# Cross-attention kernel: later Wo and key-block loads, a zeroed tile on TensorE during the first loads, high products of two row blocks first

## The reference

```
Q = split_heads(x @ Wq + bq);  K = split_heads(ctx @ Wk + bk);  V = split_heads(ctx @ Wv + bv)
scores = einsum('bhqd,bhkd->bhqk', Q, K) / sqrt(32)
attn   = softmax(scores, axis=-1)
c      = einsum('bhqk,bhkd->bhqd', attn, V), heads joined
out    = c @ Wo + bo
result = layer_norm(out + x) * gamma + beta          # eps 1e-5
x: (16, 512, 512) f32      ctx: (16, 77, 512) f32
```

## Time and profile before

| | us |
|---|---|
| median of 3 runs | 618.29 (618.0 to 619.93) |
| the profiled execution, whole | 621.88 |
| its span, first to last instruction | 620.1 |
| TensorE busy | 594.5 |
| VectorE busy | 498.2 |
| GpSimd busy | 443.5 |
| ScalarE busy | 364.0 |

### The profile page before, as it was taken

How to read it: one execution, slowest core, us unless ns; L and a number is a source line. 1 busy time by engine, 2 the same in 40 slices (tenths; PEclk the granted TensorE clock), 3 DMA queues, 4 the chain that set the end, 5 groups by cost and what they waited for, 6 DMA issues and landing times.

```text
span 620.1 us, 12039 instructions
## 1 busy us (share of the span) xinstructions
PE 594.5 (96%) x3336; PEld 432.1 (70%) x3336; DVE 498.2 (80%) x913; ACT 364.0 (59%) x674; POOL 443.5 (72%) x395
## 2 busy tenths in 40 slices
PE   5998799999999999999999999999999999999992
PEld 4876577777777777777777777777777777777562
DVE  5434288888888888888888888888888888888776
ACT  5532155466666666666666666666666666655562
POOL 1264143448888888888888888888888888888785
PEclk9999799999999999999999999999999999999997
DMA  8759968888979898979798988989897989796623
GB/s 304 275 211 223 230 142 223 223 198 195 234 200 212 218 225 216 215 203 231 190 230 206 229 218 197 231 204 228 194 245 191 223 206 228 190 230 169 168 77 128
DMA packets 93392, 129.58 MB, mean 209 GB/s; under 512 B 49936, under 2 KB 49936, under 8 KB 93360
## 3 DMA queue, kind: packets, MB, share of 16 engines
q1 hardware_dynamic: 74016, 93.80, 61.0%
q10 hardware_dynamic: 19344, 35.40, 21.9%
HBM read 53.94 MB, written 24.35 MB: 126 GB/s over the span
## 4 chain that ended last, share of the span: by engine, by line
PE 90%; SPq 4%; DMA 3%; DVE 1%; issue 1%; ACT 0%; DVEq 0%
PE p_q L612 27%; PE p_o L680 27%; PE p_s L644 11%; PE p_v L655 10%; PE p_a L630 6%; PE pk L309 5%; PE p_o L111 3%; DMA z<-nmt 1%; SPq L550 1%; SPq L545 1%; PE p_a L697 1%; DMA k_low<-ktl 1%; PE p_den L663 1%; DMA cx<-in_ctx_t 1%; SPq L491 1%
## 5 line engine op out<-in xcount | busy, mean ns | idle before, releaser
L753 ACT ACTIVATE prob<-p_s 77x512 f32<-77x512 f32 x256 | 143.8, 591 | 107.9 <-PE p_s L644 98.0
L968 DVE TENSOR_REDUCE nm<-p_a 128x4 f32<-128x308 f32 x256 | 117.3, 476 | 57.7 <-PE p_a L630 56.8
L1104 POOL TENSOR_TENSOR cl<-cxt,ch 128x512 fp32r<-128x512 f32 x64 | 83.1, 1298 | 111.3 <-ACT ch L778 111.3
L923 DVE TRANSPOSE_TENSOR_REDUCE part<-prob 96x64 f32<-96x2048 f32 x64 | 146.4, 2287 | 1.6 <-issue 1.3
L768 ACT ACTIVATE qh<-p_q,bq_col 128x512 fp32r<-128x512 f32 x64 | 44.0, 687 | 105.6 <-PE p_q L612 105.6
L612 PE MATMUL p_q<-xl,wqh 128*128 128x512 f32 x256 | 101.2, 395 | 0.0
L612 PE MATMUL p_q<-xh,wql 128*128 128x512 f32 x256 | 101.0, 395 | 0.0
L612 PE MATMUL p_q<-xh,wqh 128*128 128x512 f32 x256 | 101.0, 394 | 0.0
L644 PE MATMUL p_s<-z,ks 97*77 97x512 f32 x256 | 95.8, 415 | 5.2 <-DMA z<-nmt 5.1
L680 PE MATMUL p_o<-woh,ch 128*128 128x512 f32 x240 | 95.4, 397 | 0.2 <-POOL cl L1104 0.2
L680 PE MATMUL p_o<-wol,ch 128*128 128x512 f32 x240 | 94.6, 394 | 0.0
(11 more groups left out here) (126 smaller groups left out, 937.2 us busy)
## 6 DMA issues: line engine op xcount, KB each, us to landing
z<-qh SPq DMA_DIRECT2D x256, 128.0 KB, 3.8
z<-ql SPq DMA_DIRECT2D x124, 128.0 KB, 4.8
xn<-in_x ACTq DMA_DIRECT2D x60, 256.0 KB, 3.3
out_dram<-y SPq DMA_DIRECT2D x60, 256.0 KB, 4.2
xt<-in_x_t ACTq DMA_DIRECT2D x58, 256.0 KB, 4.7
ks<-k_high SPq DMA_DIRECT2D x32, 154.0 KB, 4.7
cx<-in_ctx_t SPq DMA_DIRECT2D x4, 616.0 KB, 5.6
k_high<-kth SPq DMA_DIRECT2D x4, 616.0 KB, 3.6
```

Source lines behind the costliest of these rows:

```text
L753: nc.scalar.activation(prob[0:S2, j, :], p_s[j % 2][0:S2, :], ACT.Exp, scale=SCALE).then_inc(prob_ready, 1)
L923: nc.vector.tensor_reduce(part[:], prob[0:KP, :, :].rearrange("p h (i r) -> p (h i) r", r=DK), AX_X, ALU.add, apply_transpose=True).then_i ...
L968: nc.vector.tensor_reduce(nm[:, t, g.k % 2:HALF:2], p_a[t % 2][:, 0:HC * S2].rearrange("p (h k) -> p h k", k=S2), AX_X, ALU.max, negate=Tr ...
L1104: nc.gpsimd.tensor_tensor(cl[:, i, g.k % NCH, :], cx[:], ch[:, i, g.k % NCH, :].bitcast(F32), ALU.subtract).then_inc(cl_ready, 1)
```

## The change

Wo blocks 0 and 1 are loaded in slot 3 and made ready in slot 4, blocks 2 and 3 in slots 5 and 6 (before: loaded ahead of slot 0 and in slot 2, made ready in slots 1 and 3). The `kb` load of the next batch moves from the second slot of a batch, ahead of z, to its third slot, behind the maxima and `v`. In the first stage DVE sets a tile of 128 x 512 f32 (a part of `y`) to zero, and TensorE multiplies it three times by its own first 128 columns as soon as that is done. The result goes to a bank that the first real product overwrites. For row blocks 0 and 1 TensorE no longer takes the three products of a tile together, but for all six tiles first high x high, which waits for `kv_high` alone, then low weights x high context, then high weights x low context. Row blocks 2 and 3 go as before, with the last two products of a tile exchanged.

```diff
-WO_SLOTS = (1, 3)
+WO_SLOTS = (4, 6)
+WARM = 3
...
+        zeros = y[:, 0, :]
...
+            nc.vector.memset(zeros, 0.0).then_inc(zeros_set, 1)
             for i in range(3 * KC):
                 low(i)
...
-            def k_products(i, kc):
+            def k_products(i, kc, terms=range(3)):
...
-                for n, (w, x) in enumerate(((wkh, cxh), (wkh, cxl), (wkl, cxh))):
+                for n in terms:
+                    w, x = ((wkh, cxh), (wkl, cxh), (wkh, cxl))[n]
...
-            for kc in range(KC):
+            pe.wait_ge(zeros_set, 1)
+            for _ in range(WARM):
+                nc.tensor.matmul(pk[0][:], zeros[:, 0:P], zeros[:], start=True, stop=True)
+            for kc in range(2):
+                for n, ready in ((0, kv_high), (1, kv_low), (2, kv_low)):
+                    for i in range(PK):
+                        if i == 0 and n != 1:
+                            pe.wait_ge(ready, 3 * kc + 2)
+                        if i == 0 and n == 1:
+                            pe.wait_ge(ready, 3 * kc + 1)
+                        if i == 1 and n != 1:
+                            pe.wait_ge(ready, 3 * kc + 3)
+                        k_products(i, kc, (n,))
+            for kc in range(2, KC):
                 for i in range(PK):
...
-            for kc in range(2):
-                load_wo(kc)
-
...
-                if g.k % NCH == 1 and g.back(1 - NCH).valid(NG):
-                    if g.back(1).is_first():
+                if g.k % NCH == 2 and g.back(2 - NCH).valid(NG):
+                    if g.back(2).is_first():
                         sp.wait_ge(kb1_zeroed, 1)
-                    load_kb(g.back(1 - NCH))
+                    load_kb(g.back(2 - NCH))
...
-                if g.back(WO_SLOTS[0] + 1).is_first():
-                    load_wo(2)
-                    load_wo(3)
+                for half in range(2):
+                    if g.back(WO_SLOTS[half] - 1).is_first():
+                        load_wo(2 * half)
+                        load_wo(2 * half + 1)
```

More of the change, by code:

```diff
@@ L153, in project_context @@
         k_summed, k_high_out = sem("k_summed"), sem("k_high_out")
-        sel_ready = sem("sel_ready")
+        sel_ready, zeros_set = sem("sel_ready"), sem("zeros_set")
+        zeros = y[:, 0, :]
         first = [part for kc in range(KC) for part in (
```

## The result

The changed kernel takes 612.95 us (median of 20 runs, 611.97 to 618.3) against 618.49 for the kernel before (20 runs, one of them an outlier of 2068.67): ratio 0.9914, 95% interval 0.9897 to 0.993. That is 5.5 us less, where 8.4 were forecast. The profiled execution took 612.02 us with a span of 610.2, 9.9 us less than the profiled one of before. So two numbers have to be explained: 9.9 in the profile, 5.5 in the median.

A forecast was written before the change was run, and what follows sets the result against it. TensorE, busy 96% of the span, was taken as the bound, improvable only where idle or at half speed. 3.1 + 3.5 + 2.8 - 1.0 = 8.4 us off 618.29 gives 609.9; range 607.3 to 614.8.

The forecast's parts named there:

- First stage, 3.1 us: Ahead of slot 0: zeroed-tile products raise the clock, real products run at full speed from 6.4; gain 3.1 us.
- The rival with the zero tile: First stage: zero tile does not raise the clock, real products run cold; total gain 5.9, giving 612.4; 7%.
- It passes through: From first stage to the end: nothing there is tied to an absolute time, so its 3.1 us gain passes whole.
- Wait for the maxima, 3.5 us: Slot 3: with Wo and kb moved, the last z<-nmt lands earlier, TensorE resumes at 67.8; gain 3.5, bounds 2.4 and 4.2.
- whether the moved loads also free xt: Slot 2 wait for qh, 1.70 us: zero if xt is freed, 0.6 if not; the sum is the same.
- Clock after the wait, 2.8 us: After slot 3's wait: idle time of 2.5 us brings no clock fall; gain 2.8, bounds 0 and 2.8.
- What is late next, 1.0 us: Maxima of pairs 1 and 2 and ScalarE's Wo waits, slots 4 to 6: charge of 1.0 us, bounds 0 and 3.
- the sign I had set myself: Prediction is wrong if a wait over 2 us shows in slots 4 to 7, or if the steady slots grow.
- From the profile to the median: Whole run: the 8.4 us gain, summed against the profiled 621.88, taken unchanged from the median 618.29, giving 609.9.
- the first rival: After slot 3's wait: clock fall is absent from timed runs or comes again; gain 5.6, giving 612.7; 18%.
- Steady part, nothing: Later batches: kb moves to a slot where SP rests, 1.94 us fit into 4.0; zero, within 0.3 us a batch.
- 2.5 us is shorter than 3.6, so no fall: Slot 3: before, the clock fell about 3.6 us after TensorE went idle; new idle time 2.5, so no fall.

The follow-up runs named there:

- first stage alone: Changed kernel with the Wo and kb loads back at their places of before; 617.29 us against 619.24 for the kernel before, ratio 0.9971.
- rows later: Changed kernel with the three broadcast rows (gamma, beta, bo) loaded in slot 6 instead of slot 5; 614.17 us, ratio 0.9903.
- loads alone: Kernel before with only the Wo and kb loads moved as in the change; 617.46 us against 619.24 for the kernel before, ratio 0.9985.

## Why the prediction held in direction and missed in size

- **First stage, 3.1 us.** Right in kind: 2.64 between the two profiles compared, 2.4 to 3.25 over all nine profiles with the three products and the new order (second key set at 20.10 to 20.92). The term was 0.5 high, because the real products on the wide tile started at 6.92 instead of 6.4: six instructions cost 5.49 us, within the 5.1 to 6.4 that I had, and the start at 1.46 was 0.15 later. From 6.92, four blocks of 3.44 us give the measured 20.7. Full speed came just after 7, between the 6.4 and 8.2 that I had; with two products it was there by 6.34. So it comes earlier or later from one execution to the next, and that I took the shorter time was in part luck. The Trainium skill, TensorE: Matmul & The Clock Gate, Part 1, has the gate follow how busy the engine is; the trace agrees in that zeros raised it (0.24 between starts from 8.19 us against 0.43 up to 12.57 before). The rival with the zero tile fell.
- **It passes through.** Right: slot 0 starts 2.64 us earlier (39.95 against 42.59), the last store of K is 4.02 us in flight both times.
- **Wait for the maxima, 3.5 us.** 4.40 measured, just over my bound of 4.2. Two sizes were off, in opposite ways. The eight z<-qh issues kept their slow pace of 5.80 us and z<-ql theirs, so the last maxima went out 0.9 us earlier beyond the first stage, not 2.2. But they were 2.02 us in flight, instead of the 4.5 in my sum (67.8 - 63.3) and the 3.8 of its short end: the nearest row I took, z<-qh at the median, is of a loaded queue, and here the transfer engines were at a share of 0.17. What I had left open beside it, whether the moved loads also free xt, the runs settle: they do (8.7 to 4.0 us in flight).
- **Clock after the wait, 2.8 us.** Right in this profile, 2.78, since the wait was 1.36 us. The price is not a constant, though. The fall of before costs 2.8 us; the others seen cost less: 1.5 in first stage alone (5.78 against 4.32 from the scores of slot 3 to slot 4) and in slot 7 of the changed kernel (5.80), 1.6 in slot 9 of rows later, and 1.3 to 1.5 for the three late ones (from slot 8 to the end are 509.9 to 510.1 us there, 508.6 without one). The profile I summed from had the dearest of them all.
- **What is late next, 1.0 us.** 0 in the profile of the result, but 3.7 in the second profile of the same kernel, and 1.0 to 2.7 in four others with the same places for Wo and the rows. The mechanism fits the one named, Wo ahead of the maxima of pair 2, as far as the order of issues shows it. By the sign I had set myself, a wait over 2 us in slots 4 to 7, the second profile (2.20 in slot 7) speaks against the prediction; the first does not. What I missed is that a wait there can bring a clock fall of its own (my bound of 3 had none), and that the three broadcast rows are under way on ScalarE's queue at that time; they were not in my sum at all.
- **From the profile to the median.** This is the step that failed, and with it the size. I took the sum, made against an execution of 621.88 us, off the median of 618.29 unchanged. The profiled execution of before was at the slow end of its own runs, that of the changed kernel near the fast end: 9.9 is 5.5 for the medians, 3.4 by which before's profile stands over its median and 0.9 by which the other stands under its own. In one set 7 of 35 runs of before had a clock of 0.993 or more, with a median of 616.48, and 25 had 0.991 or less, with 620.05. Of the changed kernel 14 of 20 had the first (612.63), 3 the second (617.52). So the fall is in most runs of before but not in all, and in a few of the changed kernel it comes again. That is the first rival (612.7 forecast, 612.95 measured), with both of its halves true in part. Its sum fits by luck as well: it takes off only the fall and leaves 5.6 us, but among the executions at 0.993 or more the change gives 3.7 to 3.9 us (612.93 against 616.63 on one chip, 612.63 against 616.48 across sets). In that class first stage alone gives 3.9 (two runs) and loads alone 0.5, so there the 3.5 us that I had for the maxima are not seen.
- **Steady part, nothing.** Right: from slot 8 (101.63 after, 111.44 before) to the end are 508.6 and 508.7 us.

Not settled: why the loads alone give only 0.5 us among the runs at a high clock (615.98, five runs, against 616.48). None of before's fast executions was profiled, so what they wait for in slot 3 is not known.

## What to carry to other kernels

A single profiled execution is a sample: before its waits are summed against a median, look where its time stands among the runs, and price a clock fall by how many runs have it and by more than one fall. Where an engine sits idle during the first loads, products on a zeroed tile bring its clock up early, and here a new order of products was worth more behind them (about 1 us) than without them (0.4 to 0.6). Of two transfers ahead of a late one, moving either brought most of the gain and moving the second added little; so test each by itself before moving both. Put them back where no due transfer stands behind them, and count all that is in flight there, from the other engines' queues too.

## What the runs showed of the hardware

- The granted clock fell in waits of 4.25 and 4.22 us, but also in one of 2.20 (second profile of the changed kernel), 0.9 us after one of 1.59 (rows later) and 1.6 to 2.5 us after waits of 0.89 to 1.23 behind the last query projection (three profiles), while waits of 2.10, 2.51 and 2.65 passed without a fall. The length of a wait alone does not decide it, and my step "2.5 us is shorter than 3.6, so no fall" would have been luck had the wait been 2.5.
- A fall cost 2.8 us in one profile and 1.3 to 1.6 in six others.
- A transfer of 4 KB was 5.55 us in flight with the transfer engines at a share of 0.85 to 1.05 and 2.02 with them at 0.17, a factor of 2.7 for the same instruction. One of 256 KB on ScalarE's queue went from 8.7 to 4.0 us when loads were moved off SP's queue.
- The profile's granted clock reads 1.00 in the first 12 us of before, while starts 0.43 us apart show 1.2 GHz there.
